# A graph attention layer: high and low parts in one matmul of 130 columns, and the s1 row spread into PSUM by TensorE

## What is computed

```python
h  = einsum('bnf,hfo->bhno', x, W)
s1 = einsum('bhno,ho->bhn', h, a1);  s2 = einsum('bhno,ho->bhn', h, a2)
e  = leaky_relu(s1[..., :, None] + s2[..., None, :], negative_slope=0.2)
attn = softmax(where(adj > 0, e, -9e15), axis=-1)
h_prime = einsum('bhnm,bhmo->bhno', attn, h)      # heads concatenated to 512
out = layernorm(x + h_prime, axis=-1)
```

## Time and profile before

| what | us |
|---|---|
| runs of the kernel before, median of 3 | 3147.84 |
| lowest and highest | 3135.4 and 3163.03 |
| the profiled execution, its own time | 3138.42 |
| its span, first to last instruction | 3136.7 |
| mean granted TensorE clock, share of full | 0.967 |

### The profile page before, as it was taken

One profiled execution on the slowest core, in us unless ns is written; L12 is line 12 of the kernel. 1 busy time (PEld: TensorE's weight loads), 2 busy tenths in 40 slices (PEclk: granted clock), 3 DMA queues, 4 the chain that ended last, 5 costly groups with the idle time before them and its releaser, 6 DMA issues.

```text
span 3136.7 us, 158793 instructions
## 1 busy us (share of the span) xinstructions
PE 2744.1 (87%) x68636; PEld 2398.0 (76%) x68636; DVE 2522.8 (80%) x3954; ACT 2419.3 (77%) x4029; POOL 827.5 (26%) x1011
## 2 busy tenths in 40 slices
PE   4898889998898898988989889998898888988886
PEld 2498876988678885888858888498884888758886
DVE  4888878887887878888788787888877877788876
ACT  2499973999658996599856998479973989739994
POOL 2522115111341113312142111521215111161211
PEclk9999999999999999999999999999999999999998
DMA  5357643576526655277442765437644556345753
GB/s 162 93 116 161 141 100 100 123 164 131 130 71 136 150 130 136 63 157 157 111 118 70 159 155 122 98 88 165 150 108 115 112 143 156 90 112 115 165 135 94
DMA packets 281338, 392.28 MB, mean 125 GB/s; under 512 B 161856, under 2 KB 161856, under 8 KB 280672
## 3 DMA queue, kind: packets, MB, share of 16 engines
q1 hardware_dynamic: 253536, 315.24, 39.9%
q0 software_dynamic: 27136, 67.12, 12.7%
HBM read 313.52 MB, written 34.14 MB: 111 GB/s over the span
## 4 chain that ended last, share of the span: by engine, by line
PE 67%; issue 13%; DVE 10%; ACT 7%; DMA 1%; SPq 1%; POOL 0%; DVEq 0%; ACTq 0%; POOLq 0%
PE ps L475 14%; PE ps L476 14%; PE ps L455 13%; PE ps L454 13%; PE ps L429 8%; ACT step L519 7%; PE ps L368 2%; DVE m_neg L731 1%; DVE y L603 1%; PE ps L386 1%; PE ps L399 1%; DVE prod L695 1%; PE ps L448 1%; DVE prod_d L698 1%; DVE m_pos L722 1%
## 5 line engine op out<-in xcount | busy, mean ns | idle before, releaser
L519 ACT ACTIVATE step<-ps,s_steep 128x512 fp8e4<-128x512 f32 x3328 | 1954.1, 726 | 289.7 <-DVE m_pos L722 246.9
L455 PE MATMUL ps<-b_lo,m_pos 128*128 128x65 f16 x16384 | 1094.3, 195 | 96.4 <-issue 95.4
L454 PE MATMUL ps<-b_hi,m_pos 128*128 128x65 f16 x16384 | 1093.7, 195 | 54.4 <-issue 36.5
L475 PE MATMUL ps<-d_hi,m_neg 128*128 128x65 f16 x16384 | 1071.9, 195 | 67.0 <-issue 61.2
L455 PEld LDWEIGHTS ps<-b_lo,m_pos 128*128 128x128 fp8e5 x16384 | 1052.3, 98 | 101.3 <-issue 101.0
L475 PEld LDWEIGHTS ps<-d_hi,m_neg 128*128 128x128 fp8e5 x16384 | 1043.6, 99 | 98.5 <-issue 97.9
L476 PE MATMUL ps<-d_lo,m_neg 128*128 128x65 f16 x16384 | 1072.7, 195 | 42.3 <-issue 42.1
L454 PEld LDWEIGHTS ps<-b_hi,m_pos 128*128 128x128 fp8e5 x16384 | 1052.5, 98 | 66.3 <-issue 66.1
L476 PEld LDWEIGHTS ps<-d_lo,m_neg 128*128 128x128 fp8e5 x16384 | 1039.1, 99 | 34.9 <-issue 33.3
L722 DVE TENSOR_TENSOR m_pos<-step,maskT 128x1024 uint32<-128x1024 uint32 x512 | 623.8, 1242 | 163.4 <-ACT step L519 130.6
L731 DVE TENSOR_TENSOR m_neg<-m_pos,maskT 128x1024 uint32<-128x1024 uint32 x512 | 602.8, 1217 | 0.0
(11 more groups left out here) (81 smaller groups left out, 1703.4 us busy)
## 6 DMA issues: line engine op xcount, KB each, us to landing
adj_in<-in_adj SPq DMA_DIRECT2D x266, 512.0 KB, 4.8
s_bc<-s_rows SPq DMA_DIRECT2D x258, 256.0 KB, 3.8
x_in<-in_x SPq DMA_DIRECT2D x144, 256.0 KB, 4.7
x_sum<-in_x POOLq DMA_DIRECT2D x128, 256.0 KB, 4.6
y<-in_x POOLq DMA_DIRECT2D x32, 1024.0 KB, 10.4
out<-y SPq DMA_DIRECT2D x32, 1024.0 KB, 7.4
maskT<-adj_cut SPq DMA_TRANSPOSE x264, 4.3
W_sb<-in_L_gnn_W SPq DMA_DIRECT2D x4, 256.0 KB, 6.8
```

Source lines behind the costliest of these rows:

```text
L454: pe.matmul(acc, mask, b_hi[:, j, h, :], start=False, stop=False)
L455: mm = pe.matmul(acc, mask, b_lo[:, j, h, :], start=False, stop=(j == JC - 1))
L475: pe.matmul(acc, mask, d_hi[:, j, h, :], start=(j == 0), stop=False)
L519: ins = nc.scalar.activation(chunk(step[qd], c, 0, BLK), ps[:, BANK_S1, :], ACT.Relu, bias=s2_steep[:, j, h:h + 1], scale=STEEP, saturate= ...
```

## The change

**One matmul for high and low.** `b_hi` and `b_lo` become the two halves of one tile `b_both` with the parts next to each other for each head, and `d_both` likewise. A matmul has 130 columns. The accumulators of a row tile are 130 columns wide, two to a bank: the positive sums take banks 0 and 1, the negative ones banks 2 and 3, for every unit. VectorE folds the two parts with a TENSOR_REDUCE over pairs, `take_pos` for the positive half (placed between `m_pos` and `m_neg` of the next unit) and `take_neg` for the negative. `m_neg` is made by one instruction of 2048 words.

**s1 by a matmul.** VectorE cuts s1 of a batch into three bfloat16 parts (`cut_s1`); TensorE turns them (`turn_s1`), ScalarE copies them to SBUF once a batch (`copy_s1`), and for each unit a matmul with a stationary selector of 96 rows spreads the sum of the three parts of the unit's row to 128 partitions (`spread_s1`), into bank 4 or 5 by the unit's parity. ScalarE no longer copies. `s1_bc` and its DMA stay for VectorE's three chunks.

**Banks moved:** H_BANKS (7, 4, 6) becomes (7, 6, 4); the mean moves from bank 4 to 6, the sum from 4 to 7.

```diff
-    H_BANKS = (7, 4, 6)
+    H_BANKS = (7, 6, 4)
+    PARTS = 3
+    S1_ROWS = PARTS * KB * H
...
-        b_hi = sb("b_hi", [P, JC, H, O1], F16)
-        b_lo = sb("b_lo", [P, JC, H, O1], F16)
-        d_hi = sb("d_hi", [P, JC, H, O1], F16)
-        d_lo = sb("d_lo", [P, JC, H, O1], F16)
+        b_both = sb("b_both", [P, JC, H, 2, O1], F16)
+        d_both = sb("d_both", [P, JC, H, 2, O1], F16)
+        b_hi, b_lo = b_both[:, :, :, 0, :], b_both[:, :, :, 1, :]
+        d_hi, d_lo = d_both[:, :, :, 0, :], d_both[:, :, :, 1, :]
...
+        S = 2 * O1
+        def slot(bank, it):
+            return ps[:, bank + it // 2, it % 2 * S:(it % 2 + 1) * S]
+        def slots(bank):
+            return ps[:, bank:bank + 2, 0:2 * S].rearrange("p k (t l c) -> p k t c l", t=2, l=2)
...
             def load_s1(u, slot):
-                sp.wait_ge(step_act, at(step_act, QUADS * (u - 1)))
-                sp.sem_inc(waited[sp.engine], 1)
                 sp.wait_ge(step_dve, at(step_dve, u - 1))
...
+            def turn_s1(n):
+                pe.wait_ge(s1_cut, 4 * (n + 1))
+                for t in range(IT):
+                    mm = pe.matmul(ps[0:S1_ROWS, BANK_PARTS, t * P:(t + 1) * P],
+                                   s1_parts[:, t, :, :, :].rearrange("p a k h -> p (a k h)"), ident_bf[:], start=True, stop=True)
+                mm.then_inc(s1_turned, 1)
+            def spread_s1(unit):
+                pe.matmul(ps[:, BANK_S1 + unit % 2, :], s1_pick[:, unit:unit + 1].to_broadcast([S1_ROWS, P]), s1_T[:],
+                          start=True, stop=True).then_inc(s1_spread, 1)
...
                     if jc == 0:
-                        pe.wait_ge(s_col_copied, b + 1)
+                        pe.wait_ge(s1_T_copied, b + 1)
+                    if jc == 2:
+                        pe.wait_ge(step_act, at(step_act, QUADS * (b * UNITS + 1)))
...
                         pe.wait_ge(pos_made, at(pos_made, QUADS * (u + 1)))
-                        pe.wait_ge(unit_read, at(unit_read, u - 1))
+                        pe.wait_ge(pos_read, at(pos_read, u))
                         for it in range(IT):
-                            acc = ps[:, 2 * hp, it * O1:(it + 1) * O1]
-                            pe.matmul(acc, ones_bf[:], tiny[:, h, :], start=True, stop=False)
+                            acc = slot(0, it)
                             for j in range(JC):
...
-                                pe.matmul(acc, mask, b_hi[:, j, h, :], start=False, stop=False)
-                                mm = pe.matmul(acc, mask, b_lo[:, j, h, :], start=False, stop=(j == JC - 1))
+                                mm = pe.matmul(acc, mask, b_both[:, j, h, :, :], start=(j == 0), stop=(j == JC - 1))
+                                if j == 0:
+                                    pe.matmul(acc[:, 0:O1], ones_bf[:], tiny[:, h, :], start=False, stop=False)
                         mm.then_inc(pos_summed, 1)
...
+                        if unit == UNITS - 2:
+                            pe.wait_ge(s1_T_copied, b + 2)
+                        spread_s1((unit + 2) % UNITS)
+                        if unit == STAT_UNIT + 1:
+                            turn_s1(b + 1)
...
-                        pe.wait_ge(neg_made, at(neg_made, QUADS * (u + 1)))
+                        pe.wait_ge(neg_made, at(neg_made, u + 1))
+                        pe.wait_ge(neg_read, at(neg_read, u))
...
-                            acc = ps[:, 2 * hp + 1, it * O1:(it + 1) * O1]
+                            acc = slot(2, it)
...
-                                pe.matmul(acc, mask, d_hi[:, j, h, :], start=(j == 0), stop=False)
-                                mm = pe.matmul(acc, mask, d_lo[:, j, h, :], start=False, stop=(j == JC - 1))
+                                mm = pe.matmul(acc, mask, d_both[:, j, h, :, :], start=(j == 0), stop=(j == JC - 1))
...
-            def compare(u, h, nth):
-                act.wait_ge(s1_loaded[h % 2], 16 * (nth + 1))
-                act.wait_ge(step_act, at(step_act, QUADS * u))
-                nc.scalar.activation(ps[:, BANK_S1, :], s1_bc[h % 2][:], ACT.Copy).then_inc(s1_copied, 1)
-                act.wait_ge(s1_copied, u + 1)
+            def compare(u, h):
+                act.wait_ge(s1_spread, u + 1)
...
-            def take_unit(u, h, it0):
+            def take_pos(u, h):
+                dve.wait_ge(pos_summed, at(pos_summed, u + 1))
+                dve.wait_ge(att_made, at(att_made, u - 1))
+                V.tensor_reduce(total[hp][:], slots(0), AX.X, ALU.add).then_inc(pos_read, 1)
+            def take_neg(u, h, it0):
                 dve.wait_ge(unit_done, at(unit_done, u + 1))
-                V.tensor_tensor(neg_part[:], neg, r, ALU.mult).then_inc(neg_scaled, 1)
+                V.tensor_reduce(neg_part[:], slots(2), AX.X, ALU.add).then_inc(neg_read, 1)
+                dve.wait_ge(neg_read, at(neg_read, u + 1))
+                V.tensor_tensor(neg_part[:], neg_part[:], r, ALU.mult).then_inc(neg_scaled, 1)
                 dve.wait_ge(neg_scaled, u + 1)
-                V.tensor_tensor(total[hp][:], pos, neg_part[:], ALU.add).then_inc(unit_read, 1)
+                V.tensor_tensor(total[hp][:], total[hp][:], neg_part[:], ALU.add).then_inc(total_made, 1)
...
+            def cut_s1(n):
+                s1 = s_col[:].rearrange("p (k t) s -> p t k s", t=IT)[:, :, :, 0:H]
+                V.tensor_copy(s1_parts[:, :, 0, :, :], s1).then_inc(s1_cut, 1)
+                V.tensor_tensor(s1_rest[:], s1, s1_parts[:, :, 0, :, :], ALU.subtract).then_inc(s1_cut, 1)
+                V.tensor_copy(s1_parts[:, :, 1, :, :], s1_rest[:]).then_inc(s1_cut, 1)
+                V.tensor_tensor(s1_parts[:, :, 2, :, :], s1_rest[:], s1_parts[:, :, 1, :, :], ALU.subtract).then_inc(s1_cut, 1)
...
-            def make_neg(u, h, mask, qd):
+            def make_neg(u, h, mask):
...
+                V.tensor_tensor(words(m_neg[hp][:]), words(m_pos[hp][:]), words(mask[:]), ALU.bitwise_xor
+                                ).then_inc(neg_made, 1)
...
                 for qd in range(QUADS):
                     make_pos(u, h, mask, qd, first_of_block)
-                for qd in range(QUADS):
-                    make_neg(u, h, mask, qd)
+                if before is not None:
+                    take_pos(u - 1, before)
+                make_neg(u, h, mask)
```

95 lines of the change are left out of this document (66 added, 29 removed).

## The result

The changed kernel takes 3098.46 us (median of 4 runs, 3097.05 to 3100.6) beside 3152.14 for the kernel before on the same chip: a ratio of 0.9852, 95% interval 0.981 to 0.9893, 1.5% faster. The forecast was 3138, no difference that can be measured. The profiled execution took 3097.49 us, with a span of 3095.8.

The account below looks back on a forecast made before the run. VectorE was to bound every unit after the change: -14 us in the batch stretches, +5 outside, so 3138.4 - 9 = 3129 us profiled, given as a 3138 median; own range 3090 to 3185, wider range 2990 to 3235.

Parts of the forecast that it names:

- VectorE becomes the bound: Kernel after: VectorE bounds all units at about 91% busy, its waits for TensorE outside first units near zero.
- rivals 1 and 5: VectorE's folds: 1, reduces cost by outputs, 2997 us, chance 0.14; 5, the step between halves costs extra, 3414, chance 0.08.
- rival 4: TensorE: the 98 ns weight load no longer hides, over 3.5 us more a unit, about 4000 us; chance 0.02.
- +1.28 us a unit: VectorE's added work: take_pos +0.62, take_neg +0.74, m_neg in one instruction -0.08 us.
- 250 + 131 us of waiting: VectorE's old waits for TensorE and ScalarE in the eight batch stretches, claimed filled by 248 x 1.28 = 317 us of work.
- 0.35 and 0.35: Chances for the measured time: 0.35 faster by over about 1% (31 us), 0.35 the same; slower had 0.30.
- no single one is the bound everywhere: Kernel before: three engines close together, matrix engine 87% of the span, VectorE 80%, ScalarE 77%.
- Fits under that lead: TensorE leads VectorE by 4.2 us a unit, so a 2.5 us pause or 3.64 us of fp32 scores costs nothing.
- Rival 3: Second half of a unit: TensorE's lead runs out, 2 us in 5 units a batch, 80 us, 3218; chance 0.13.
- TensorE's terms: 130-column matmuls 57 ns apart, TensorE about 8.1 us a unit and idle 2, instruction traffic near 4.7 MB.
- 9.2 becomes 8.3: ScalarE's us a unit: without its copy of s1 and the wait behind it, some 0.95 us less.
- Rival 2: VectorE's new work is hidden and ScalarE was the bound: 243 us less, 2895; chance 0.05.

Follow-up runs that it names:

- e3: Kernel after the change with both folds reading only the high parts, 260 PSUM words in place of 520: 3004.53 us, ratio 0.954 to the kernel before.
- e2: Changed kernel with the s1 spread kept, but matmuls of 65 columns, two sets of banks and no folds: 3189.99 us, ratio 1.0115 to the kernel before.
- e7: Kernel before with every matmul by a low part left out, halving TensorE's mask stream: 3007.57 us, ratio 0.9603.
- e4: Changed kernel with 15 of 16 matmuls of 130 columns made as two of 65 again, folds and spread kept: 3274.59 us, ratio 1.0396 to the kernel before.
- e12: e4 with each part padded to 66 elements so the low part starts at a multiple of 4 bytes: 3270.25 us, ratio 1.0454 to the kernel before.
- e1: Changed kernel with ScalarE's copy of s1 back and TensorE's spread gone, wide matmuls and folds kept: 3126.87 us, ratio 0.9954 to the kernel before.
- e9: e2 with high and low parts in tiles of their own, as before the change: 3175.88 us, ratio 1.0146 to the kernel before.
- e5: Changed kernel with one of VectorE's three compare chunks given to ScalarE: 3068.69 us, ratio 0.9799 to the kernel before.

## Why the prediction was right and wrong

**VectorE becomes the bound.** Right. Its share is 91% (2825 us, forecast 2855), its waits for TensorE outside a batch's edge are gone, and e3 showed that two thirds of the work taken from it come off the time. The two reduces take 693 and 691 ns (0.70), the multiply 429 (0.43): rivals 1 and 5 fell with these rows, and rival 4 with the matmuls' spacing. The unit stretches of the batches, 304 to 317 us before, are 307.0 to 307.3 in seven of the eight.

**The step that failed in the sum: "+1.28 us a unit".** VectorE's busy time in the eight stretches was put at 2038 + 317 + 12 = 2367 us and is 2327.6, 39 less. Idle time was put at 76 + 38 = 114 and is 119; outside the stretches it was +5 and is +7. So the miss of 32 us on the profiled execution (3129 against 3097.5) is in that one term. By line in the stretches, with overlaps counted once, most of it is `take_neg`: it takes 160 us more than `take_unit` did, 0.65 us a unit, where 0.74 (184 us) was put. `take_pos` (152 us, put at 154) and `m_neg` (-17, put at -20) came as forecast; `cut_s1` took 7.5 us in place of 12, the other instructions of a batch some 5 less, and 512 `m_pos`, which the change did not touch, 8 less (623.8 us over the span before, 615.7 after).

The cause is for the larger part an overlap that the prediction allowed for `take_pos` and left out here: an instruction of VectorE that follows another without a wait starts 0.08 us before its end (1715.30 against 1714.71 + 0.68), and behind a wait it doesn't. 145 waits of `take_unit` for TensorE and 101 of `m_pos` for ScalarE in these stretches became 1 and 14, and 231 x 0.08 = 18 us. The overlaps counted in the trace give about that: 12 of `take_neg`'s 23 us and the 8 of `m_pos`. Another 0.03 us a unit (7 us) is a short gap between two of `take_neg`'s instructions, which was put into its busy time. The rest of the 23 us is rounding.

**Which case was likeliest.** I called 250 + 131 us of waiting "filled by 317 us of new work" and got a difference of two large numbers near each other, with a sign that hung on 40 us. In such a sum a term that is off by 12% turns "same" into "faster". The chances (0.35 and 0.35) said so; the number did not. That 3098 still lies in the forecast's own range is in part luck: the range was given as 0.15 us a unit either way, which is 256 x 0.15 = 38 us, 3100 to 3176, and not 3090 to 3185.

**What bounded the kernel before.** The prediction said "no single one is the bound everywhere", and treated 9.2 us of ScalarE as nearest. The runs show it was TensorE with its pauses: 9.03 us occupied and 0.97 of "issue" leave 0.05 of the interval of 10.06. Part of ScalarE's 9.2 was a misreading: 0.28 us behind its copy is what it waits in a unit where the copy is what it waits for last, and the view of waits has 155 such units, 42.8 us, or 0.17 a unit. e2 relieved ScalarE (8.95 to 8.58) and put 0.32 us on TensorE: the kernel became slower. e7 relieved TensorE alone: 4% faster, until ScalarE took over. I read the pauses from one example of 2.47 us, where the view by line and form would have summed them to 235 us.

**"Fits under that lead."** For the kernel after this holds. Its second halves end 3.7 us on average before VectorE reads them (forecast 4.2), and less than 1 us before in 9 of 248 units; and it has next to no pauses: 8, all at a batch's first unit, where TensorE waits for GpSimd's last low part. For the pauses of before it does not: in e4 the same lead is 1.5 us on average, and less than 1 us in 141 units; e4 and e12 have the lead of a single set of banks and the old stream, and lose 176 and 172 us. So the argument that TensorE's gain is worth only the disappearance of VectorE's waits was right in the outcome, but those waits could vanish only with the wide matmul's shorter work and halved stream. Rival 3 was given 80 us; the runs with the old stream lose twice that, TensorE's longer work included.

**TensorE's terms.** Right in the main: the spacing of the 130-column matmuls is 57.0 ns in the median (forecast 57), the traffic 4.85 MB (4.7). TensorE is occupied 8.65 us a unit and not 8.1, and idles 1.2 and not 2; its lead was long enough for that to cost nothing. The Trainium skill's figure of about 81 ns for a load and matmul pair at 128 columns (TensorE: Matmul & The Clock Gate, Back-to-back issue gap) is not met here at 57.

**ScalarE's terms.** "9.2 becomes 8.3": it is 8.60 occupied. Of that, 0.16 is the compare of unit 2, which now runs later: 68 more of the step ACTIVATEs fall into the stretches, at 0.58 us each. The rest is not placed. This cost nothing, as it then waits 160 times for `m_pos` (204 us, 0.8 us a unit where 1 to 1.5 was forecast). The late compare of unit 2 cost at most 0.9 us a batch, with everything else between batches in it, within the bounds of 0 and 1.

**Rival 2** (ScalarE was the bound, 2895) fell twice: e2 shows that relief of ScalarE alone is worth nothing, e1 that it is worth 28 us beside the wide matmul.

**Not tried:** `m_neg` in one instruction, the third part of the change, was in every kernel here but before and e7, and never undone alone. By its rows it takes 0.07 us a unit off VectorE.

## What the runs showed of the hardware

TensorE's pauses go with the length of its instruction stream. Before, the instruction queue moved 545 packets of about 16 KB, one per 5.8 us, and 194 of the 207 pauses end 1.2 to 1.65 us after the end of such a packet; 165 of 179 in e2, 165 of 175 in e4, 188 of 200 in e9 and 169 of 180 in e12. Of moments picked at random in the trace of before, 8% lie so. This is counted from the traces:

```
                 packets   pauses   of these end 1.2-1.65 us after a packet
before             545       207      194
after              296         8        0
e7, no low parts   289        12        4
e4, two matmuls    536       175      165
```

Of the 8 and the 12, 8 each are the waits for GpSimd at a batch's first unit; the 4 others of e7 take 0.3 to 0.5 us each. So TensorE pauses where 256 matmuls with their loads go by in a unit, and hardly where there are 128. That it waits for the delivery of these packets is an inference from the match in time; no run changed the number of instructions alone. The nearest pair is before and after: half the instructions, TensorE occupied 9.03 and 8.65 us a unit, but with 1.2 us of waiting for VectorE after. What makes a packet late was not tried.

A TENSOR_REDUCE over pairs of words 65 apart in PSUM costs what one over neighbours does: 693 ns for 520 words, beside 692 for 512 neighbouring words; 260 words in e3 take 421.

Two streams of 65 columns from one shared tile are spaced 29.2 and 33.3 ns, from own tiles 30.4 each. The reason stays open; an even start does not change it.

Open too is why ScalarE's and VectorE's balance gives so little: by its trace e5 took 0.39 us a unit from VectorE, and the unit's interval fell by 0.12.

## What to carry to other kernels

Sum the idle time called "issue" over all forms of an engine's instructions before calling it free: here 235 us of it made TensorE the bound that its busy time alone did not show. A wider matmul that halves the number of instructions can be worth more than the matmul time it saves: 176 us with VectorE's folds in both kernels (e4), and still 92 us with the folds counted against it (e2); and a matmul put in an engine's place is only a relief where TensorE is not the bound (28 us gained in the one case, 1 to 2% lost in the other). After such a change rebalance: moving compare chunks from the new bound gave another 0.9%.
